# Sorting experts by load and preparing their weights inside the first expert stage

## The reference

```
def ffn(x):                      # Wr 256x8, W1 8x256x1024, W2 8x1024x256
    e = argmax(softmax(x @ Wr)); p = max(softmax(x @ Wr))
    h = gelu(x @ W1[e] + b1[e])
    return p * (h @ W2[e] + b2[e])

def ssm(u):                      # diagonal complex recurrence, 128 states
    h_t = a_disc * h_{t-1} + B_disc @ u_t
    return Re(C @ h_t)

x = x + 0.5 * ffn(layernorm(x))
x = x + ssm(layernorm(x))
x = x + 0.5 * ffn(layernorm(x))
```

## Time and profile before

| | us |
|---|---|
| median of 3 runs | 741.01 |
| lowest and highest run | 734.8, 749.26 |
| span of the profiled execution | 743.5 (the page gives no other time of it) |
| TensorE busy in the span | 589.5 (79%) |
| VectorE busy | 531.1 (71%) |
| ScalarE busy | 396.8 (53%) |
| GpSimd busy | 330.0 (44%) |

### The profile page before, as it was taken

One profiled execution on the slowest core, in us unless ns is written; L12 is line 12 of the kernel. 1 busy time (PEld: TensorE's weight loads), 2 busy tenths in 40 slices (PEclk: granted clock), 3 DMA queues, 4 the chain that ended last, 5 costly groups with the idle time before them and its releaser, 6 DMA issues.

```text
span 743.5 us, 18466 instructions
## 1 busy us (share of the span) xinstructions
PE 589.5 (79%) x6396; PEld 518.0 (70%) x6396; DVE 531.1 (71%) x1204; ACT 396.8 (53%) x879; POOL 330.0 (44%) x310
## 2 busy tenths in 40 slices
PE   5960149999999899994477878139999999999997
PEld 5950138998888787893245657129998778988886
DVE  5869967778886775784499993927776666766675
ACT  4877846565554555552336653107555546546463
POOL 0031183555545453531477881162555454554532
PEclk9555559999999999998658895558999999999999
DMA  8993031111111111113102211030111111111210
GB/s 276 374 375 122 5 99 31 40 45 43 49 45 38 35 51 37 38 30 99 51 29 90 80 57 57 1 103 19 44 51 44 36 50 36 45 41 36 50 36 2
DMA packets 34872, 51.86 MB, mean 70 GB/s; under 512 B 6747, under 2 KB 27933, under 8 KB 34528
## 3 DMA queue, kind: packets, MB, share of 16 engines
q1 hardware_dynamic: 24800, 31.90, 12.6%
q0 software_dynamic: 9984, 18.79, 9.0%
HBM read 37.95 MB, written 14.55 MB: 71 GB/s over the span
## 4 chain that ended last, share of the span: by engine, by line
PE 68%; DVE 18%; issue 7%; DMA 3%; ACT 2%; POOL 1%; SPq 1%; ACTq 0%; POOLq 0%; DVEq 0%
PE bank L1065 31%; PE bank L1082 9%; PE bank L1083 9%; PE bank L1084 9%; PE bank L982 4%; PE bank L1041 3%; DVE stats L580 3%; DVE weights_arena L613 2%; PE bank L976 2%; DMA weights_arena<-L_attn_u 2%; DVE weights_arena L920 1%; DVE weights_arena L757 1%; DVE weights_arena L917 1%; DVE weights_arena L942 1%; DVE ev L927 1%
## 5 line engine op out<-in xcount | busy, mean ns | idle before, releaser
L519 ACT ACTIVATE weights_arena<-bank,b1t,inv 128x128 f32<-128x128 f32 x624 | 228.4, 467 | 211.2 <-PE bank L1065 161.2
L1065 PE MATMUL bank<-weights_arena 128*128 128x128 f16 x3744 | 239.2, 222 | 23.5 <-issue 17.5
L1065 PEld LDWEIGHTS bank<-weights_arena 128*128 x3744 | 220.6, 99 | 39.8 <-issue 37.0
L1082 PE MATMUL bank<-weights_arena 128*128 x624 | 170.2, 273 | 1.2 <-issue 1.0
L1083 PE MATMUL bank<-weights_arena 128*128 x624 | 170.1, 273 | 1.3 <-issue 1.1
L1084 PE MATMUL bank<-weights_arena 128*128 x624 | 170.1, 273 | 0.9 <-issue 0.6
L816 DVE TENSOR_SCALAR weights_arena<-weights_arena,hscale 128x512 f16<-128x512 f32 x156 | 76.8, 492 | 83.6 <-ACT weights_arena L519 77.4
L819 DVE SCALAR_TENSOR_TENSOR weights_arena<-weights_arena,hscale 128x512 f16<-128x512 f32 x156 | 117.3, 752 | 5.6
L375 POOL DMA_INDIRECT recf<-records,sorti x78 | 81.4, 1043 | 23.8 <-issue 23.8
L381 POOL DMA_INDIRECT out<-weights_arena,sorti x39 | 39.5, 1013 | 112.7 <-DVE weights_arena L835 99.8
L381 POOL DMA_INDIRECT x_after_ffn<-weights_arena,sorti x39 | 40.6, 1040 | 105.3 <-DVE weights_arena L835 95.8
(11 more groups left out here) (181 smaller groups left out, 702.0 us busy)
## 6 DMA issues: line engine op xcount, KB each, us to landing
weights_arena<-L_ffn_W SPq DMA_DIRECT2D x16, 1024.0 KB, 12.6
weights_arena<-L_attn_u SPq DMA_DIRECT2D x8, 512.0 KB, 9.9
weights_arena<-x_after_ffn SPq DMA_DIRECT2D x8, 512.0 KB, 4.8
x_after_ssm<-weights_arena SPq DMA_DIRECT2D x8, 512.0 KB, 3.1
weights_arena<-L_ffn_b SPq DMA_DIRECT2D x2, 1024.0 KB, 4.4
recf<-records,sorti POOLq DMA_INDIRECT x78
weights_arena<-L_attn_u,sorti POOLq DMA_INDIRECT x39
x_after_ffn<-weights_arena,sorti POOLq DMA_INDIRECT x39
```

Source lines behind the costliest of these rows:

```text
L519: last = act.activation(hb[q % 2][:, f, :], src, ACT.Gelu, bias=b1t[:, bass.ds(e * FC + f, 1)], scale=inv1[:, bass.ds(e, 1)])
L1065: last = pe.matmul(acc[:, f * P:(f + 1) * P], weights[wpart * DC + d], xts[q % 2][:, xpart, d, :], start=(n == 0), stop=(n == 5))
L1082: pe.matmul(acc, hs[q % 2][:, 0, f, :], high, start=(f == 0), stop=False)
```

## The change

- The bias b1 is no longer loaded and turned in the entry, and x is loaded in one go. No weight is loaded or prepared before the routing is known.
- In `route_count` VectorE ranks the experts by their number of tiles, the largest first, and writes the ranks (`rank`), the tile offsets in that order and the experts by rank (`order`, semaphore `order_done`). SP reads `order` into a register and loads the expert of rank 0 and 1, the others each when the low parts of the rank two below are done. b1 comes with each expert, in pieces of 4 bytes, and b2 in eight loads. Weights lie in SBUF by rank, and `eid` holds ranks, in both stages.
- Rank 0 is prepared at the end of routing. Rank r from 1 to 7 is prepared within tiles 4(r-1) to 4r-1 of the first expert stage: ScalarE does one row sum or one high part behind the gelu of each tile (`prepare`), VectorE one half of a low part in each tile, and once in four tiles the weight scales, the bounds and the product scales of that expert alone. Since the largest experts come first, rank r owns no tile below 4r.
- In the expert stages VectorE's order changes: the high and the low pieces of split_x and split_h are apart, with the second piece of split_x behind the first piece of split_h, and `result` is cut in two; TensorE's product2 waits for the first of them.
- The doublings and readouts of the rotation tables are made in the entry, before the wait for the logits.
- Areas of SBUF are laid out anew.

The core of the diff (twelve leading blanks cut; helper declarations and the layout of areas left out):

```diff
-LAG = 4
+LAG = 2
...
 def raw(e, which):
-a = big[:, (2 * e + which + LAG) * WB:(2 * e + which + LAG + 1) * WB].bitcast(F32)
+n = 2 * e + which
+if n + LAG < NW:
+    a = big[:, (n + LAG) * WB:(n + LAG + 1) * WB].bitcast(F32)
+else:
+    a = view(late_raw + (n + LAG - NW) * WB // 4, WB // 4)
 return a if which == 0 else a.rearrange("p (f d) -> p f d", f=FC)
...
+def gbank(e, step):
+return 6 + step if e else 5
...
-sp.dma_start(b1raw, A["L0_ffn_b1"].rearrange("e (c p) -> (e c) p", p=P)).then_inc(par_in, 16)
-for c in (1, 2):
+for c in range(1, NC):
     load_x(c)
-for e in range(E):
-    for c in {1: (3, 4, 5), 2: (6, 7)}.get(e, ()):
-        load_x(c)
-    if e >= E - 2:
-        sp.wait_ge(a_t, (e - E + 3) * NC // 2)
-        sp.wait_ge(a_stats, (e - E + 3) * NC // 2)
-    for which, W in enumerate((W1, W2)):
-        at = (2 * e + which + LAG) * WB
-        sp.dma_start(big[:, at:at + WB].bitcast(F32).rearrange("p (c f) -> p c f", c=W.shape[2]), W[e]) \
-            .then_inc(wload[2 * e + which], 16)
+def load_expert(r):
+    e = sp.value_load(order[0:1, r:r + 1], min_val=0, max_val=E - 1)
+    sp.dma_start(raw(r, 0).rearrange("p (c f) -> p c f", c=DC),
+                 W1[bass.ds(e, 1)].rearrange("o p c f -> (o p) c f")).then_inc(wload[2 * r], 16)
+    sp.dma_start(raw(r, 1), W2[bass.ds(e, 1)].rearrange("o p c d -> (o p) c d")).then_inc(wload[2 * r + 1], 16)
+    sp.dma_start(b1t[:, r * FC:(r + 1) * FC], B1[bass.ds(e, 1)].rearrange("o p c -> (o p) c"),
+                 allow_slow_non_contiguous=True) \
+        .then_inc(wload[2 * r + 1], 16)
...
-    sp.dma_start(b2b, A["L0_ffn_b2"].rearrange("e d -> (e d)").partition_broadcast(P)) \
-        .then_inc(S[ph]["b2in"], 16)
+    for r in range(E):
+        e = sp.value_load(order[0:1, r:r + 1], min_val=0, max_val=E - 1)
+        sp.dma_start(b2b[:, r * D:(r + 1) * D],
+                     A["L0_ffn_b2"][bass.ds(e, 1)].rearrange("o d -> (o d)").partition_broadcast(P)) \
+            .then_inc(S[ph]["b2in"], 16)
...
+sp.wait_ge(order_done, 1)
+load_expert(0)
+load_expert(1)
 store_records(1)
 load_b2(1)
+for r in range(2, E):
+    sp.wait_ge(w_lo, 2 * r - 2)
+    load_expert(r)
...
 def row_sums(e, which):
-    act.wait_ge(wload[2 * e + which], 16)
-    src = raw(e, which)
-    to = dump if which == 0 else dump.rearrange("p (f d) -> p f d", f=FC)
     n = 2 * e + which
+    act.wait_ge(wload[n], 16 if which == 0 else 32)
         act.wait_ge(w_sum, n)
-    act.activation(to, src, ACT.Abs, accum_out=wsum[:, n:n + 1]).then_inc(w_sum, 1)
+    to = dump if which == 0 else dump.rearrange("p (f d) -> p f d", f=FC)
+    act.activation(to, raw(e, which), ACT.Abs, accum_out=wsum[:, n:n + 1]).then_inc(w_sum, 1)
...
-    if e >= 2:
+    if n >= LAG:
         act.wait_ge(w_lo, n - LAG + 1)
...
-turned_x(0)
-turned_x(1)
-row_sums(0, 0)
-turned_x(2)
-row_sums(0, 1)
-turned_x(3)
-high_part(0, 0)
-high_part(0, 1)
-turned_x(4)
-row_sums(1, 0)
-row_sums(1, 1)
-turned_x(5)
-high_part(1, 0)
-row_sums(2, 0)
-turned_x(6)
-high_part(1, 1)
-row_sums(2, 1)
-turned_x(7)
-for e in range(2, E):
-    high_part(e, 0)
-    if e + 1 < E:
-        row_sums(e + 1, 0)
-        row_sums(e + 1, 1)
-    high_part(e, 1)
-    if e == 3:
-        odds(1)
+for c in range(NC):
+    turned_x(c)
+odds(1)
+def prepare(k):
+    if 0 <= k < 4 * (E - 1):
+        (row_sums if k % 4 < 2 else high_part)(1 + k // 4, k % 2)
...
     act.activation(spare[:], mhalf[:, 0:1], ACT.Gelu)
+    if ph == 1:
+        row_sums(0, 0)
+        row_sums(0, 1)
+        high_part(0, 0)
+        high_part(0, 1)
     act.wait_ge(s["sorted_sb"], 1)
-    act.wait_ge(inv_done, 1)
...
+    if ph == 1:
+        prepare(0)
+        prepare(1)
...
+        if ph == 1 and q % 4 == 0 and q < 4 * E:
+            act.wait_ge(inv_done, q // 4 + 1)
...
+        if ph == 1:
+            prepare(q + 2)
...
 def weight_scales(e):
     two = slice(2 * e, 2 * e + 2)
+    mag = bound[:, e, 0:2]
     dve.wait_ge(w_sum, 2 * e + 2)
+    dve.wait_ge(wload[2 * e + 1], 32)
+    dve.tensor_reduce(bound[:, e, 2:3], b1t[:, e * FC:(e + 1) * FC], AX, ALU.max, apply_absolute_value=True)
...
+def low_part(e, which, half):
+    part_of = slice(half * DC * F // 2, (half + 1) * DC * F // 2) if which == 0 else slice(half * FC // 2, (half + 1) * FC // 2)
     dve.wait_ge(w_hi, n + 1)
-    dve.scalar_tensor_tensor(lo, raw(e, which), wscale[:, n:n + 1], hi, ALU.mult, ALU.subtract) \
-        .then_inc(w_lo, 1)
+    last = dve.scalar_tensor_tensor(lo[:, part_of], raw(e, which)[:, part_of], wscale[:, n:n + 1],
+                                    hi[:, part_of], ALU.mult, ALU.subtract)
+    if half == 1:
+        last.then_inc(w_lo, 1)
...
-link(dve.tensor_copy(b1t[:], bank[5][:, 0:E * FC]))
-link(dve.tensor_reduce(bound[:, NW:NW + E], b1t[:].rearrange("p (e c) -> p e c", c=FC), AX, ALU.max,
-                       apply_absolute_value=True))
...
+def bounds_up(e):
+    dve.wait_ge(g_t, e + 1)
+    link(dve.tensor_reduce(gtop[0:3, e:e + 1], bank[gbank(e, 0)][0:3, 256:256 + P], AX, ALU.max))
+    dve.tensor_scalar(gbc[0:3, :], iota_r[0:3, :], 0.0, gtop[0:3, e:e + 1], ALU.mult, ALU.add).then_inc(g_max, 1)
+def product_scales(e):
+    one_of = slice(e, e + 1)
+    g1, g2, gb = (gall[:, e, k:k + 1] for k in range(3))
+    dve.wait_ge(g_all, e + 1)
+    link(dve.tensor_copy(gall[:, e, :], bank[gbank(e, 1)][:, 400:403]))
+    dve.tensor_scalar(inv1[:, one_of], g1, 1.0 / SX, None, ALU.mult)
+    dve.reciprocal(ginv[:, e, :], gall[:, e, :])
+    link(dve.scalar_tensor_tensor(hpow[:, one_of], g1, 2 * HB * TOP, gb, ALU.mult, ALU.add))
+    link(dve.tensor_scalar(hpow[:, one_of].bitcast(I32), hpow[:, one_of].bitcast(I32), EXPONENT, None,
+                           ALU.bitwise_and))
+    dve.scalar_tensor_tensor(inv2[:, one_of], g2, 1.0 / TOP, hpow[:, one_of], ALU.mult, ALU.mult)
+    dve.scalar_tensor_tensor(xscale[:, one_of], bound[:, e, 0:1], SX, ginv[:, e, 0:1], ALU.mult, ALU.mult)
+    link(dve.scalar_tensor_tensor(hscale[:, one_of], bound[:, e, 1:2], TOP, ginv[:, e, 1:2], ALU.mult, ALU.mult))
+    link(dve.reciprocal(hpow[:, one_of], hpow[:, one_of]))
+    link(dve.tensor_tensor(hscale[:, one_of], hscale[:, one_of], hpow[:, one_of], ALU.mult))
+    dve.sem_inc(inv_done, 1)
...
+    dve.tensor_tensor(cnt, ends, cnt, ALU.subtract)
     link(dve.tensor_copy(tiles, tend.bitcast(I32)))
-    link(dve.tensor_tensor_scan(tend, one[:].to_broadcast([P, E]), tiles, 0.0, ALU.mult, ALU.add))
-    link(dve.tensor_tensor(tiles, tend, tiles, ALU.subtract))
-    link(dve.tensor_tensor(cnt, ends, cnt, ALU.subtract))
-    link(dve.scalar_tensor_tensor(base, tiles, float(P), cnt, ALU.mult, ALU.subtract))
+    if ph == 1:
+        link(dve.scalar_tensor_tensor(key[:], tiles, 2.0 * E, rev[:], ALU.mult, ALU.add))
+        link(dve.tensor_tensor(ahead[:], key[:].unsqueeze(1).to_broadcast([P, E, E]),
+                               key[:].unsqueeze(2).to_broadcast([P, E, E]), ALU.is_gt))
+        link(dve.tensor_reduce(rank[:], ahead[:], AX, ALU.add))
+        dve.tensor_tensor(ahead[:], ahead[:], tiles.unsqueeze(1).to_broadcast([P, E, E]), ALU.mult)
+        link(dve.tensor_tensor(ahead_t[:], rank[:].unsqueeze(1).to_broadcast([P, E, E]),
+                               iota_r[:, 0:E].unsqueeze(2).to_broadcast([P, E, E]), ALU.is_equal))
+        dve.tensor_reduce(base, ahead[:], AX, ALU.add)
+        link(dve.tensor_tensor(ahead_t[:], ahead_t[:], iota_r[:, 0:E].unsqueeze(1).to_broadcast([P, E, E]),
+                               ALU.mult))
+        link(dve.tensor_reduce(order_f[:], ahead_t[:], AX, ALU.add))
+        dve.tensor_copy(order[:], order_f[:]).then_inc(order_done, 1)
+        link(dve.tensor_tensor(tend, base, tiles, ALU.add))
+        dve.tensor_tensor(rank_step[:, 0:E - 1], rank[:, 1:E], rank[:, 0:E - 1], ALU.subtract)
+        link(dve.scalar_tensor_tensor(base, base, float(P), cnt, ALU.mult, ALU.subtract))
+    else:
+        link(dve.tensor_tensor_scan(tend, one[:].to_broadcast([P, E]), tiles, 0.0, ALU.mult, ALU.add))
+        link(dve.tensor_tensor(tiles, tend, tiles, ALU.subtract))
+        link(dve.scalar_tensor_tensor(base, tiles, float(P), cnt, ALU.mult, ALU.subtract))
...
+    if ph == 1:
+        link(dve.tensor_reduce(eidf, ntc, AX, ALU.add))
+        dve.tensor_scalar(eid[:], eidf, float(E - 1), None, ALU.min)
+    else:
+        link(dve.tensor_tensor(ntc[:, :, 0:E - 1], ntc[:, :, 0:E - 1],
+                               rank_step[:, 0:E - 1].unsqueeze(1).to_broadcast([P, NT, E - 1]), ALU.mult))
+        link(dve.tensor_reduce(eidf, ntc[:, :, 0:E - 1], AX, ALU.add))
+        dve.tensor_scalar(eid[:], eidf, rank[:, 0:1], None, ALU.add)
...
+    def split_x(q, part_of):
+        if part_of == 0:
+            experts[q] = dve.value_load(eid[0:1, q:q + 1], min_val=0, max_val=E - 1)
+            dve.wait_ge(s["turned"], q + 1)
+            if q >= 2:
+                dve.wait_ge(s["m1"], q * 2 - 2)
+        sc = xscale[:, bass.ds(experts[q], 1)]
+        if part_of == 0:
```

(130 more changed lines are left out.)

108 lines of the change are left out of this document (35 added, 73 removed).

## The result

In the first comparison the changed kernel took 748.6 us (median of 4 runs, 743.68 to 748.74), the kernel before 737.9 beside it (732.59 to 749.26): a ratio of 1.0148, 95% interval 1.0084 to 1.0211. It moved the other way than forecast. Two later groups compared both kernels again, and the sign did not stay: 1.0033 (0.9935 to 1.0132) in group 3, and 1.0007 (0.9982 to 1.0031) in group 4, on a chip where both kernels take about 700 us. So two questions follow: where the entry's gain went, and what made the first comparison worse than even.

A forecast was written before the change was run, and what follows sets the result against it. Bound: TensorE in the expert stages; in the entry TensorE up to the logits, then VectorE. Terms: -24.2 entry, +3.5 first tiles, +8.4 stage 1, +3 stage 2 = -9.3, from 741.01 to 731.7 us; range 716 to 751.

The forecast's parts named there:

- Entry: Up to the first product: logits at 45.9, indices 70.3, first split 78.3, first product 79.8; gives 24.2 us.
- rival (4): Entry: the ranked weights come late, 6 us more, 738 us; chance 0.10.
- First scatter: First tiles of stage 1: two delays add 3.5 us (bounds 0 and 6), first scatter at 99.8.
- Tiles with preparation: Stage 1 up to tile 27: VectorE needs 6.2 us a tile against TensorE's 5.90, costing 8.4 us (bounds 0 and 28).
- Rival (1): Stage 1: VectorE keeps pace, its true load under 5.9 us a tile; 720 us; chance 0.20.
- Rival (2): Tiles 0 to 27: preparation costs more than the entry gave, from 6.53 us a tile; 751 us at 6.9; chance 0.18.
- moving the rotation tables out of the stage: Doublings and readouts move to the entry: hidden there at no cost, hidden in the stage before, so they bring nothing.
- GpSimd: Stage 1: half low parts add up to 1.3 us a tile to its issues, 3.9 to 5.2, still under 5.9.
- loses nothing in its steady pace: Expert stage 2: weights kept in rank order, steady pace unchanged, no cost.
- the same code: SSM stage: code unchanged, no cost counted.
- The start: Start of stage 2: second product waits behind the first split of h, 3 us lost (bounds 0 and 5.4).
- Rival (3): Entry: TensorE's clock rises and the logits chain takes half, 14 us less, 718 us; chance 0.07.

The follow-up runs named there:

- e13b: Changed kernel without the low parts of ranks 1 to 7 (high parts multiplied twice instead), on a chip without slow pairs: 681.9 us, ratio 0.9722.
- e14: Changed kernel with most of ScalarE's row sums of ranks 1 to 7 left out (an eighth of the elements, scaled by 8): 738.3 us.
- b1: Kernel before, unchanged, run again on a chip without slow pairs: 700.8 us.
- e3: Kernel before with the changed kernel's VectorE order in expert stage 2 only: 743.3 us (735.48 to 751.95).
- e5: Changed kernel; in stage 2 the second product waits again for the residual of tile q-2: 699.9 us, ratio 1.0009 to the kernel before.
- e8: Changed kernel; stage 2 keeps the new start, then VectorE's order of before: 700.1 us, ratio 0.9994 to the kernel before.
- e9: Changed kernel; in stage 2 direct transfers from SyncE replace GpSimd's indirect ones: 704.3 us, ratio 1.0065 to the kernel before.
- e10: Changed kernel; in stage 2 both parts of a tile's x made together, parts of h apart: 699.7 us, ratio 0.998 to the kernel before.
- a1: Changed kernel, unchanged, run again on a chip without slow pairs: 701.9 us, ratio 1.0007 to the kernel before.
- run 97: Not a run number: 97 counts the matmuls from 20 to 40 us in the first comparison's profiled run of the changed kernel, 748.68 us.
- e2: Changed kernel; at both expert stages' start the second part of tile 1's x precedes the first split of h: 728.2 us (722.03 to 747.46).
- e9b: Changed kernel with stage 2's indirect transfers replaced by direct ones from SyncE, on a chip without slow pairs: 708.1 us, ratio 1.0066.
- e12: Changed kernel; VectorE's old order in stage 2; in stage 1 tile 1's second x part before the first split of h: 730.5 us, ratio 0.9847.
- e13: Changed kernel without the low parts of ranks 1 to 7 (high parts multiplied twice instead), on a chip with slow pairs: 729.0 us, ratio 0.98.
- b0: Kernel before, unchanged, run again on a chip with slow pairs: 743.9 us over ten runs.

## Why the prediction was wrong

**Entry: right within 3 us, in part by luck.** Logits 45.9 against 46.45 (VectorE waited 9.43 us there: the tables are hidden, as said), indices 70.3 against 70.49, first split 78.3 against 78.51. The first product is at 81.90 for 79.8: TensorE turns tile 1 ahead of it, and ScalarE normalises that tile only at 79.88. The order was ready at 54.08 as forecast; ScalarE's second sum ends at 65.97, 3 us before the scales' instructions, so rival (4) did not come about. First scatter 102.42 for 99.8. The 0.5 us that I took off TensorE's start did not come: its first work is at 7.51 for 6.67, behind another load. And the logits of the same or nearly the same entry are copied at 42.87 to 49.19 in the other traces, so that they came within 0.6 us here is luck.

**Tiles with preparation: mis-sized twice.** My sum was 6.4 us a tile; I took 6.2, hoping for closed gaps. It is 25.6 for four, 6.4, in every copy of the changed kernel on both kinds of chip. The second error is the yardstick: 5.90 is no speed of TensorE. On chips without slow pairs the kernel before runs tiles at 5.5, and stage 1 costs +19.2 there; in the first comparison only +7.3, because the slow pairs had already cost the kernel before that time. That this is close to my +8.4 is luck: the tiles with preparation cost 12.1, and the tiles behind them, for which I had nothing, gave 4.8. The e13b run bears out VectorE as the bound, e14 clears ScalarE's sums. Rival (1) is refuted: VectorE never kept pace. Rival (2) was not reached at its 6.53 us a tile; but against 5.5 in place of 5.9 the preparation did cost about what the entry gave, which comes close to rival (2).

I had also put moving the rotation tables out of the stage at nothing. Before, the distances behind tiles 8 to 16, where the doublings stand, are 5.77 to 6.93 us on either kind of chip, and in b1 the first 26 distances add up to 146.0 us, 2.5 more than 26 of 5.52. So they were not wholly hidden; no run takes them out alone.

**GpSimd: hardly lengthened.** I allowed 1.3 us a tile for issues held up beside a half low part. The page's groups after (mean ns of one in the middle):

```profile
L407 POOL DMA_INDIRECT x_after_ffn<-weights_arena,sorti x39 | 39.8, 1021 | 120.3 <-DVE weights_arena L888 114.3
...
L401 POOL DMA_INDIRECT weights_arena<-L_attn_u,sorti x39 | 39.8, 1020 | 20.9 <-issue 11.6 <-DVE sorti L835 9.3
```

Beside whole low parts single issues took 3.03 and 2.77 us; the stage's mean is 1.02 with halves of 1.28 us. Of the 103 issues between 100 and 330 us, 28 overlap a half low part in the record and take 1.09 us in the mean; the other 75 take 1.01. By the rule of the Trainium skill that I weighed there ("SBUF — State Buffer", section "SBUF: two separate sides") I had estimated a mean of up to 1.45; the trace does not show that, and it changed nothing in the sum.

**The step that failed:** stage 2 "loses nothing in its steady pace". It lost 8.6 us in the run profiled, with five more slow pairs, and the SSM stage, "the same code", 2.3. The start was as forecast, 2.9 for 3. In the sum, -9.3 was forecast and +3.4 measured; of these 12.7 us 8.6 are stage 2's pace, 2.6 the first scatter (-18.1 for -20.7), 2.7 the SSM stage and routing, and stage 1 gave 1.1 back. The other 7 us between the medians lie outside the two profiles and stay unexplained. But stage 2's loss is not a fixed cost: the same kernel lost 3.9 in stage 2 against the one before in group 3 (229.4 for 225.5), and 0.3 in group 4. Where there are no slow pairs the step that failed is stage 1's cost, 19.2 for 8.4. I had read TensorE's 46.69 of 50 us in the earlier trace rows as its pace, and didn't ask why an engine with its inputs ready leaves 3 us.

**What stays open.** Why a chip has slow pairs, and what starts one. That VectorE's new order always brings them is refuted by e3's 215.7 us, and the kernel before has them too; that it makes them more likely is neither shown nor ruled out. e5, e8, e9 and e10 would have told the start, the wait and GpSimd's transfers apart, but met chips without any. Whether TensorE's instructions reach it late is a rival that no run tests; the pages of both kinds of chip list the same 0.90 MB on the instruction queue q8. Nor is it settled why the first comparison had 743 to 749 in all its four runs and group 3's had 730 to 752.

**The clock.** Rival (3) did not come about: the entry stayed at 0.50. It was also the wrong thing to price: in a1 the granted clock is 1.00 from 20 to 40 us, and the logits come at 48.60, not 14 us earlier. My reading of the earlier trace rows was off by one slice, the 5s begin in the second. The Trainium skill, "TensorE: Matmul & The Clock Gate", section "What's actually happening", has sustained work bring 2.4 GHz; 20 us of TensorE without idle at 0.50 don't show it here.

## What to carry to other kernels

Ask of the engine that you take for the bound whether its pace is its own: find two neighbouring tiles that run without a break and use their time, not the stage's mean, as what added work is weighed against. Work moved off a serial entry into a stage where its engine is already at 84% (VectorE, 41.79 of 50 us in b1) can come back at full price, here 19 us against 17 to 22 won. And run both kernels on more than one chip before believing one per cent.

## What was not expected of the hardware

The granted clock of the record does not tell the rate of the entry's fp32 work. In this changed kernel (a1) TensorE is granted 1.00 from 12 to 16 us and issues 21 matmuls in it:

```profile
12.00:16.00 4.00, 4.00 (x21) 4.00 (x21) 2.88 (x23) 0.89 (x2) 0.57 (x1) 1.00 1.10 348
```

in e5, whose entry is the same code, 38:

```profile
12.00:16.00 4.00, 4.00 (x38) 4.00 (x38) 3.07 (x22) 1.97 (x4) 0.50 (x1) 1.00 1.08 342
```

From 20 to 40 us a1 has 98 at 1.00, the first comparison's run 97 at 0.50. The logits are copied at 48.60, 43.49 and 46.45 in a1, e5 and that run. Over all traces with the changed entry, the five with 1.00 from 20 to 40 us (a1, e2, e9b, e12, e13) have their logits last, at 48.49 to 49.19, and those with 0.50 at 42.87 to 46.45. In a1's ten runs those with a mean granted clock of 0.93 took 703.6 to 704.0, the others 697.7 to 703.5.

The same program differs by 40 us between chips (700 and 741 to 744). Between the traces b0 and b1 of the kernel before it is 38.4 us: 3.4 up to the first scatter, 11.2 in stage 1, 4.3 between the stages and 19.5 in stage 2. In the slow pair shown above TensorE has breaks though its inputs are there, and an increment after the first product reaches ScalarE some 5 us late, with the granted clock at 1.00 in that window. The cause is not known.
